# Draining a graph layer's row sums by a hand-written order on VectorE, ScalarE and GpSimd

## What is computed

```python
# graph layer, h = _ln(x)
mask = (adj > 0)
agg = mask @ h / max(sum(mask, axis=1), 1)
x = x + relu(concat(h @ W_self + b_self, agg @ W_nb + b_nb) @ W_comb + b_comb)
# mixture of experts, f = _ln(x), 8 experts, the best 2 of each row
logits = f @ Wg + bg
topk_scores, topk_idx = top_k(logits, 2);  w = softmax(topk_scores)
y_e = gelu(f @ W1[e] + b1[e]) @ W2[e] + b2[e]
x = x + sum over the two chosen e of w * y_e
```

## Time and profile before

| | |
|---|---|
| median of 3 runs | 503.56 us (502.27 to 506.07) |
| the profiled execution | 508.38 us, of it the span of the engines 505.0 us |
| busy, of the span | PE 436.5 us (86%), DVE 371.1 (73%), POOL 334.5 (66%), ACT 259.7 (51%) |
| main loop over the sums | until 335.6 us |
| drain and table | 335.6 to about 356 us |
| expert loop | about 356 to 486 us |
| last sums and writes | to 505 us |

### The profile page before, as it was taken

One profiled execution on the slowest core, in us unless ns is written; L12 is line 12 of the kernel. 1 busy time (PEld: TensorE's weight loads), 2 busy tenths in 40 slices (PEclk: granted clock), 3 DMA queues, 4 the chain that ended last, 5 costly groups with the idle time before them and its releaser, 6 DMA issues.

```text
span 505.0 us, 12812 instructions
## 1 busy us (share of the span) xinstructions
PE 436.5 (86%) x4214; PEld 384.7 (76%) x4214; DVE 371.1 (73%) x1056; ACT 259.7 (51%) x403; POOL 334.5 (66%) x348
## 2 busy tenths in 40 slices
PE   5789999889999889999979969964899999997710
PEld 5678988778888778988858858863799999996610
DVE  2898754577878977798569489766777777779972
ACT  2666872245543524344434443233588888886620
POOL 3498586165666877778658756366788788885570
PEclk9999999999999979999989979985799999999985
DMA  8997899889996999899999997196865556598665
GB/s 222 278 302 230 214 234 286 223 247 264 275 278 181 311 265 257 245 276 291 298 279 275 291 301 216 43 297 209 286 199 174 174 173 186 174 324 346 195 218 166
DMA packets 48687, 122.47 MB, mean 243 GB/s; under 512 B 10601, under 2 KB 19693, under 8 KB 47600
## 3 DMA queue, kind: packets, MB, share of 16 engines
q1 hardware_dynamic: 26736, 64.09, 44.6%
q0 software_dynamic: 16144, 50.49, 33.8%
q10 hardware_dynamic: 5744, 7.08, 5.1%
HBM read 96.52 MB, written 26.93 MB: 244 GB/s over the span
## 4 chain that ended last, share of the span: by engine, by line
DVE 34%; PE 16%; ACT 15%; DMA 13%; issue 10%; POOL 8%; ACTq 2%; DVEq 1%; POOLq 1%; SPq 0%
DMA wst<-in_L_ffn_W_dram 11%; PE bank L1245 7%; ACT stage L771 7%; DVE maskT L845 5%; DVE stage L1129 5%; ACT stage L776 4%; POOL rs L633 3%; DVE x_sb L930 2%; DVE xh L928 2%; DVE w L982 2%; DVE st L934 2%; PE bank L1236 2%; ACT xh L725 2%; PE bank L1237 2%; PE bank L1362 2%
## 5 line engine op out<-in xcount | busy, mean ns | idle before, releaser
L1236 PE MATMUL bank<-z_flat,maskT 128*128 128x257 f16 x1024 | 232.9, 278 | 8.5 <-issue 8.5
L1237 PE MATMUL bank<-z_lo,maskT 128*128 128x256 f16 x1024 | 232.7, 277 | 0.0
L1236 PEld LDWEIGHTS bank<-z_flat,maskT 128*128 128x128 fp8e4 x1024 | 101.9, 100 | 22.9 <-issue 9.0
L651 POOL DMA_INDIRECT pair_out<-rows,enum x78 | 93.6, 1199 | 33.3 <-issue 21.3
L1237 PEld LDWEIGHTS bank<-z_lo,maskT 128*128 128x128 fp8e4 x1024 | 101.8, 99 | 13.2
L676 ACT ACTIVATE mask<-stage,m 128x2048 fp8e4<-128x2048 int32 x32 | 64.1, 2002 | 58.7 <-DMA stage<-in_adj_dram,gidx 47.5
L584 POOL DMA_INDIRECT dispatched<-rows,slot x64 | 65.0, 1016 | 29.4 <-issue 18.2
L573 POOL DMA_INDIRECT stage<-in_adj_dram,gidx x64 | 65.7, 1027 | 26.1 <-issue 13.6
L633 POOL TENSOR_TENSOR rs<-ve,mhalf 128x1 f32<-128x1 f32 x32 | 39.0, 1220 | 49.9 <-DVE ve L939 49.8
L725 ACT ACTIVATE xh<-x_sb,nb,rs 128x256 f32<-128x256 f32 x32 | 19.2, 599 | 100.7 <-POOL nb L635 80.0
L1342 PE MATMUL bank<-stage,w 128*128 128x256 f16 x468 | 59.8, 279 | 4.8 <-DVE stage L1114 4.8
(11 more groups left out here) (179 smaller groups left out, 607.8 us busy)
## 6 DMA issues: line engine op xcount, KB each, us to landing
stage<-in_adj_dram SPq DMA_DIRECT2D x256, 128.0 KB, 6.4
stage<-dispatched SPq DMA_DIRECT2D x39, 260.0 KB, 3.2
wst<-in_L_ffn_W_dram ACTq DMA_DIRECT2D x16, 256.0 KB
z_lo<-pair_out SPq DMA_DIRECT2D x4, 1024.0 KB, 7.8
dispatched<-pad SPq DMA_DIRECT2D x15, 260.0 KB, 5.2
out_dram<-x_sb SPq DMA_DIRECT2D x28, 128.0 KB
maskT<-pair_out SPq DMA_DIRECT2D x3, 1024.0 KB, 9.4
x_sb<-in_x_dram ACTq DMA_DIRECT2D x6, 256.0 KB, 11.3
```

The costliest lines, as they stand in the source:

```text
L651: gp.indirect_dma_start(out=yp_dram[:, :], out_offset=bass.IndirectOffsetOnAxis(ap=enum[:, a, s:s + 1], axis=0), in_=ysb[:, a, s, :], in_o ...
L1236: mm(acc[u % 2][:, 0:D + 1], a, z_hi[:, i, :], start=(i == 0), stop=False)
L1237: last = mm(acc[u % 2][:, 0:D], a, z_lo[:, i, :], start=False, stop=(i == NT - 1))
```

## The change

The kernel's steps end at step 31 on VectorE and ScalarE and at s = 31 on GpSimd, and what is left is called in an order written by hand. The bodies of the helpers (`low`, `quotient`, `normalise_again`, `transposed`, `powers_of_row`) are those of the old steps. Line numbers of the kernel after differ from those of before by up to forty.

```diff
@@ GpSimd: powers and sends (before, lines 623 to 644)
+            def powers_of_row(t):
+                pool.wait_ge(s_ve2, t + 1)
+                gp.tensor_tensor(rs[:, t:t + 1], ve[:, t:t + 1], mhalf[:, 0:1], ALU.pow).then_inc(s_rs2, 1)
...
-            LAST_POWERS = NT + X1
-            sent = 0
-            for s in range(GATE_STEPS + 1):
-                if s > HOT and s % B == (HOT + 1) % B and (s - HOT) // B < NG - 1:
+            for s in range(NT):
+                if s > HOT and s % B == (HOT + 1) % B:
                     powers_of_e((s - HOT) // B)
-                if s == LAST_POWERS:
-                    powers_of_e(NG - 1)
-                if 0 <= s - X1 < NT:
-                    t = s - X1
+                if s >= X1:
+                    powers_of_row(s - X1)
...
-                for _ in range(1 if s < NT - B else 2):
-                    if sent < B * ((s - SLOT + (s == LAST_POWERS - 1)) // B + 1):
-                        dispatch(sent)
-                        sent += 1
+                if s >= SLOT:
+                    dispatch(s - SLOT)
+            sent = NT - SLOT
+            for t in (NT - 3, NT - 2):
+                powers_of_row(t)
+                if t == NT - 2:
+                    powers_of_e(NG - 2)
+                dispatch(sent)
+                sent += 1
+            powers_of_row(NT - 1)
+            dispatch(sent)
+            powers_of_e(NG - 1)
+            for t in range(sent + 1, NT):
+                dispatch(t)
@@ ScalarE (before, line 749)
-            steps(act, main_step, 3, NT + LOGIT, tail=1)
+            steps(act, main_step, 3, NT)
+            normalise_again(NT - 4)
+            transposed(NT - 5)
+            normalise_again(NT - 3)
+            transposed(NT - 4)
+            expert_hi(E - 1)
+            normalise_again(NT - 2)
+            transposed(NT - 3)
+            transposed(NT - 2)
+            normalise_again(NT - 1)
+            transposed(NT - 1)
@@ VectorE (before, lines 951 and 1102)
-                if t == NT + SLOT - 2 * B - 1:
-                    slots(NG - 2)
-                elif u % B == SLOT % B and live(known, SLOT) and t != NT + SLOT - 2 * B:
+                if u % B == SLOT % B and live(known, SLOT):
...
-            steps(dve, main_step, 4, NT + HOT - B + 1, tail=1)
+            steps(dve, main_step, 4, NT)
+            low(NT - 4)
+            quotient(NT - 3)
+            expert_scales(E - 1)
+            quotient(NT - 2)
+            low(NT - 3)
+            choose(NG - 2)
+            low(NT - 2)
+            quotient(NT - 1)
+            slots(NG - 2)
+            low(NT - 1)
+            expert_lo(E - 1)
+            choose(NG - 1)
@@ VectorE, ahead of the expert loop (before, line 1159)
-            for t in range(NT + HOT - B + 1, GATE_STEPS):
-                main_step(t, t, t)
+            slots(NG - 1)
```

More of the change, by code:

```diff
@@ L335, in gnn_moe_kernel @@
         EMAX, ESCALE, ESPLIT, PM = 3, 4, 5, 2
-        GATE_STEPS = NT + SLOT - B + 1
         def steps(eng, step, peel, end, total=None, tail=0):
@@ L716, in _, with normalise_again, transposed @@
             load_expert(0)
+            def normalise_again(i):
+                act.wait_ge(s_nb2, i + 1)
+                if i >= 2:
+                    act.wait_ge(s_lo2, i - 1)
+                apart(act)
+                sc.activation(xh[:, i % 2, :], flat(x_sb, i), ACT.Identity, bias=nb2[:, at(i)], scale=rs[:, at(i)]).then_inc(s_xh2, 1)
+                act.wait_ge(s_xh2, i + 1)
+                apart(act)
+                sc.copy(row16[:, at(i), 0:D].rearrange("p o d -> p (o d)"), xh[:, i % 2, :]).then_inc(s_hi2, 1)
+            def transposed(j):
+                act.wait_ge(s_tp2, j + 1)
+                if j:
+                    act.wait_ge(s_lgp, j)
+                apart(act)
+                sc.copy(xT[:, :], tp2[:, :]).then_inc(s_xT2, 1)
             def main_step(t, u, known):
                 if live(known, NORM):
[L720 to L734 removed]
+                    normalise_again(t - NORM)
+                if live(known, LOGIT):
+                    transposed(t - LOGIT)
                 if u % B == ESPLIT % B and live(known, ESPLIT):
@@ L909, in _, with low, quotient @@
                     const_row()
+            def low(i):
+                dve.wait_ge(s_hi2, i + 1)
+                v.tensor_tensor(row16[:, at(i), D:2 * D].rearrange("p o d -> p (o d)"), xh[:, i % 2, :],
+                                row16[:, at(i), 0:D].rearrange("p o d -> p (o d)"), ALU.subtract).then_inc(s_lo2, 1)
+            def quotient(j):
+                r, p = j % 4, acc[j % 2]
+                dve.wait_ge(s_mm, j + 1)
+                v.tensor_scalar(sdeg[:, r:r + 1], p[:, D:D + 1], 1.0, scw[:, 4:5], ALU.max, ALU.mult).then_inc(s_dg, 1)
+                dve.wait_ge(s_dg, 2 * j + 1)
+                v.reciprocal(rdeg[:, r:r + 1], sdeg[:, r:r + 1]).then_inc(s_dg, 1)
+                dve.wait_ge(s_sfc, j // B + 1)
+                dve.wait_ge(s_dg, 2 * j + 2)
+                v.scalar_tensor_tensor(tsum[:, r % 2, :], p[:, 0:D], rdeg[:, r:r + 1], x_row(j), ALU.mult, ALU.add).then_inc(s_ts, 1)
+                dve.wait_ge(s_ts, j + 1)
+                v.scalar_tensor_tensor(flat(x_sb, j), tsum[:, r % 2, :], 0.0, flat(x_sb, j), ALU.max, ALU.add).then_inc(s_x1, 1)
+                dve.wait_ge(s_x1, j + 1)
+                apart(dve)
+                v.bn_stats(st6[:, r, :], flat(x_sb, j)).then_inc(s_s2, 1)
+                dve.wait_ge(s_s2, 2 * j + 1)
+                apart(dve)
+                v.bn_aggr(mv2[:, r, :], st6[:, r, :]).then_inc(s_s2, 1)
+                dve.wait_ge(s_s2, 2 * j + 2)
+                v.tensor_scalar(ve[:, at(j)], mv2[:, r, 1:2], EPS, XS ** -2, ALU.add, ALU.mult).then_inc(s_ve2, 1)
             def main_step(t, u, known):
                 if live(known, NORM):
-                    i = t - NORM
-                    dve.wait_ge(s_hi2, i + 1)
-                    v.tensor_tensor(row16[:, at(i), D:2 * D].rearrange("p o d -> p (o d)"), xh[:, (u - NORM) % 2, :],
-                                    row16[:, at(i), 0:D].rearrange("p o d -> p (o d)"), ALU.subtract).then_inc(s_lo2, 1)
+                    low(t - NORM)
                 m = turned_in(t)
@@ L920, in main_step @@
                 if live(known, X1):
[L921 to L939 removed]
+                    quotient(t - X1)
                 m = made_in(t)
```

39 lines of the change are left out of this document (2 added, 37 removed).

## The result

The kernel after took 500.46 us (median of 20 runs, 495.99 to 503.11), the kernel before beside it 504.47 (20 runs). The ratio is 0.9916, with a 95% interval from 0.9892 to 0.9940: 4.2 us less, between 3.0 and 5.4. The forecast was 4.1. On two of the four chips of the experiments (e1 to e4, and e8 to e11) a stall of TensorE lengthens the expert loop of every kernel, before too, by some 17 us in some runs and some 50 in the others; a ratio there comes from the runs with the smaller stall where a kernel has more than one, and e10 and e11 have only runs with the larger.

What follows compares the result with a forecast made beforehand. The bound was taken as a drain chain through VectorE, GpSimd and ScalarE starting at late quotient 31. Gains of 3.8 + 0.3 = 4.1 us from the 503.56 median gave 499.5 us; forecast 498.3 to 501, wider range 497.2 to 503.0.

Steps and rivals of the forecast that it cites:

- three signs of being wrong: Sum 31 ending elsewhere, TensorE waiting for a load in the expert loop, or GpSimd's last scatter not 4 us earlier.
- Powers 29, 2.5 us earlier: Drain, GpSimd: with two of four sends gone ahead of them, the powers of tile 29 start 2.5 us earlier.
- Quotient 30 directly behind the scales, low part 30 ready ahead of the sum: Drain, VectorE: quotient 30 moves ahead of low part 29 to 329.4; low part 30 ends at 335.1.
- Quotient 31 at its sum, 3.8: Drain, VectorE: quotient 31 starts directly behind its sum, at 335.7 instead of 339.51, 3.8 us gained.
- Low part of the weights at no cost: Drain, VectorE: expert 7's low part, moved behind low part 31, fits in the 1.96 us wait before choice 7.
- With that cover gone it would cost 1.3: Drain, VectorE: without the wait ahead of choice 7, the low part of expert 7's weights would cost 1.3 us.
- Powers of e at the gap, 0.3: Drain, GpSimd: the last powers of e go ahead of sends and start at the logit gap; slots 7 gain 0.3 us.
- GpSimd no earlier, and nobody waits for it: Expert stage: sixteen later sends leave GpSimd no earlier; tile 9's load is in time by 0.3 us, scatter lag absorbed.
- the first rival: Expert loop: every second send held up, TensorE waits 2.4 us at tile 9, gain only 1.7, 501.9 us; 17%.
- the slower one: Expert stage: each of sixteen sends held up by a whole 0.75 us, 7.6 us lost, 511.2 us; 4%.
- takes up the 4: Near the end: GpSimd's 11.2 us of idle waiting for ScalarE absorbs the scatters' lag of some 4 us.
- The clock rival: First expert tiles: TensorE's clock rises sooner, 1.8 us more gained, 5.9 in all, 497.7 us; 13%.

Runs made afterwards that it cites:

- e1: VectorE and ScalarE in the changed kernel's order, GpSimd in the order of before; ratio to before 0.9986 (0.9940 to 1.0031).
- e4: Changed kernel with the low part of expert 7's weights moved behind the last choice; no usable ratio, slots of group 7 at 12.81 us behind sum 31.
- e8: The kernel of e1 run again for its time, on a chip with the stall; no usable ratio, quotient 31 at 3.58 us behind sum 31.
- e11: Changed kernel with unused matrix products in TensorE's drain waits and twelve more ahead of the third expert tile; ratio 1.0868, which is the stall.
- e10: Changed kernel with eight unused GpSimd powers between the last powers of e and the last sixteen sends; ratio 1.0837, which is the stall.
- e2: GpSimd in the changed kernel's order, VectorE and ScalarE in the order of before; ratio to before 1.0018 (0.9979 to 1.0058).
- e12: The kernel of e10 run again: changed kernel plus eight unused GpSimd powers ahead of the last sixteen sends; 505.70 us against 504.73, ratio 1.0022.
- e5: Changed kernel with three small unused GpSimd products ahead of the last sixteen sends; 498.70 us against 504.09, ratio 0.9914.
- e6: Changed kernel with eight small unused GpSimd products ahead of the last sixteen sends; 499.00 us against 504.09, ratio 0.9916.
- e7: Changed kernel with unused matrix products in TensorE's idle stretches of the drain and first expert step; 500.10 us against 504.09, ratio 0.9910.

## Why the prediction was right

Forecast 4.1 us less and 499.5; measured 4.2 (3.0 to 5.4) and 500.46 beside a before of 504.47. By the traces' places it is 3.78: 4.05 at the transposes of tile 2, 0.41 lost in that tile, 0.14 won behind tile 9. That forecast and measurement meet to 0.1 us is luck; that they meet within a microsecond is the chain. Of the three signs of being wrong one came true, sum 31 ends 2.6 us earlier than in before's trace, which is why all places are counted from it. TensorE waits for no load, and GpSimd's last scatter is 3.8 earlier (485.15 after 491.54 before, each from its sum 31).

1. **Powers 29, 2.5 us earlier.** Measured 2.51. e1 shows that without GpSimd's new order, of which this is the first effect, VectorE's is worth nothing.
2. **Quotient 30 directly behind the scales, low part 30 ready ahead of the sum.** In time from sum 31 I had quotient 30 at -6.2 and the start of low part 30 at -0.9; they are at -6.28 and -1.13.
3. **Quotient 31 at its sum, 3.8.** Measured 3.85. VectorE waits 0.77 for the sum, so that much is spare ahead of it. e2 shows where it comes from: the sends give 2.6 of it, VectorE's order the rest.
4. **Low part of the weights at no cost.** Right, with 0.64 of the wait left over as I had it (0.56). **"With that cover gone it would cost 1.3" was wrong**: 2.6 at the slots, 2.3 at tile 2 (e4). I had priced VectorE's time alone and had not asked who waits for the weights; it is TensorE, for its first expert tile.
5. **Powers of e at the gap, 0.3.** The slots gained 4.31 where quotient 31 gained 3.85, so 0.46, and they are at 10.25 where I had 10.5. But the transposes of tile 0 wait for neither and gained 3.83, and of the 0.46 the transposes of tile 2 kept 0.2 (4.05).
6. **GpSimd no earlier, and nobody waits for it.** The last send is 0.4 later than before. Two of the sixteen behind the powers of e are long (1.19 at 353.95 and 1.38 at 357.97, together 0.65 more than 0.96 each); the third long one (338.35) stands ahead of the wait of 1.50 and costs nothing. So the first rival's "every second send held up" didn't come true, and the 0.97 at 348.08 that I had set against the slower one says nothing, since VectorE has no instruction of line 1129 there. The tightest point, tile 9, I had in time by 0.3. It is in time by 4.2, because I took the load's issue from before, where it came 34.5 behind sum 31, and the slowest landing, 4.2; it was issued at 32.6 and landed in 2.7. Why the load followed the start of the last send by 5.7 us in before (364.44, 370.15) and by 3.4 in after isn't shown. With TensorE 0.5 later than forecast: 0.3 + 1.9 + 1.5 + 0.5 = 4.2. The rival "sends late, TensorE waits at tile 9" is a real mechanism with a threshold, and e12 shows it beyond that threshold.
   The lag of the scatters was absorbed in the wait for ScalarE, as said, but **"takes up the 4" was 3.2**: these waits fell from 11.2 us to 8.0. In the loop GpSimd doesn't catch up, as forecast, 28 tiles in 85.2 us:

```profile
POOL pair_out L658 <- ACT rows L784: 8.0, 7, 2.2
```

```profile
L658 POOL DMA_INDIRECT pair_out<-rows,enum x56 | 68.1, 1216 | 17.1 <-issue 16.8 <-ACT rows L784 0.3
```

**The clock rival** was to give 1.8 more and gave nothing; tile 2 took 0.4 more. The clock did rise sooner (at 347.3), but TensorE then stood idle around the table (0.93 and 1.05 us) and it fell again for tile 2, which took 4.74 us (349.41 to 354.15) against 4.33 before. That is the step from 4.05 to 3.64 in the table. With the same order of work there the tile took 4.74 in e5, 4.48 in e12 and 5.81 in e6, so the 0.4 is within what one execution differs from the next by, and its sign isn't shown.

What remains open: whether keeping the clock up through tile 2 gives its 1.4 us back, and what the two halves are worth in measured time rather than in places of the trace.

## What to carry to other kernels

A reordering on one engine can be worth nothing until the engine that feeds it is reordered too: follow the wait, and ask where it will stand next. When work is pushed back off the critical path, find the one consumer that gets it last and compute its slack from issue and landing, since beyond the slack one pays the wait and, as in e12, a tile at the lower clock as well. And measure a drain from the event that starts it: between two single executions the spans mixed 2.6 us from the main loop into a gain of 3.8.

## What I had not expected of the hardware

**A GpSimd send that starts more than 0.1 us inside a VectorE instruction with two inputs in SBUF ends some 0.86 us behind it.** e12 shows it cleanly, because its scatters drift past VectorE's line 1172 (the line 1129 of before). First VectorE, then GpSimd:

```profile
384.42 0.75 DVE L1172 SCALAR_TENSOR_TENSOR stage<-stage,shs 128x512 f16<-128x512 f32 x1 [1.63 <-ACT stage L803]
387.48 0.75 DVE L1172 SCALAR_TENSOR_TENSOR stage<-stage,shs 128x512 f16<-128x512 f32 x1 [0.72 <-ACT stage L803]
390.55 0.75 DVE L1172 SCALAR_TENSOR_TENSOR stage<-stage,shs 128x512 f16<-128x512 f32 x1 [0.72 <-ACT stage L803]
```

```profile
384.11 0.99 POOL L661 DMA_INDIRECT pair_out<-rows,enum  x1 [0.30 <-issue]
...
387.99 1.11 POOL L661 DMA_INDIRECT pair_out<-rows,enum  x1 [0.30 <-issue]
...
390.69 1.47 POOL L661 DMA_INDIRECT pair_out<-rows,enum  x1 [0.30 <-issue]
...
393.76 1.47 POOL L661 DMA_INDIRECT pair_out<-rows,enum  x1 [0.30 <-issue]
```

The scatter at 384.11 starts before VectorE's instruction and takes its usual 0.99, though it overlaps it. The one at 387.99 starts inside (387.48 to 388.23) and ends at 389.10; that at 390.69 starts inside (390.55 to 391.30) and ends at 392.16. Both end 0.87 and 0.86 behind. From 390.69 on every second scatter is caught, two take 3.07 us, and that is TensorE's time for a tile: the two engines lock. This is why the mean of a scatter was 1.229 in the earlier trace rows, and why GpSimd, which could make two in 2.58 us, doesn't catch up by 0.5 us a tile. Between 369.89 and 386.69, where VectorE's instruction first is missing (TensorE waits) and then never has a scatter start inside it, fourteen scatters in a row took 0.99 to 1.00 each.

It isn't any VectorE instruction that does it. Line 1162 of after has one of its two tiles in PSUM (`bank`), and the scatter at 375.02, inside it (374.74 to 375.48), took 0.99. A `tensor_tensor` with both inputs in SBUF does it too: the longest scatter of after, 1.87 at 480.40, starts inside one of 1.21 at 480.20 and ends 0.86 behind it. And a send that starts in the first 0.1 us of line 1169 isn't held up; VectorE's instruction is then a little longer. VectorE, then GpSimd, in after:

```profile
360.84 0.80 DVE L1169 SCALAR_TENSOR_TENSOR stage<-stage,shs 128x512 f16<-128x512 f32 x1 [0.73 <-ACT stage L800]
```

```profile
360.92 0.96 POOL L583 DMA_INDIRECT dispatched<-rows,slot  x1 [0.30 <-issue]
```

The Trainium skill (SBUF — State Buffer, "Who interferes with whom") says that a VectorE instruction with two SBUF inputs contends with a GpSimd instruction that reads SBUF, and that whichever issues first holds the port while the other waits. The rows agree on the first, and on the second where VectorE is first. Where the scatter is first they don't: VectorE's instruction at 384.42 starts inside the scatter of 384.11, takes its usual 0.75, and starts 0.14 behind the end of the ScalarE instruction that it waits for, as the one at 390.55 does with no scatter beside it. The 3.1 us that the Trainium skill has for a send starved of descriptor writes (SBUF — State Buffer, "A bandwidth-pool intuition that's wrong (but worth ruling out)") are seen in no row here.

**TensorE's clock falls for less than I thought.** Idle stretches of 1.49 and 1.02 us around a single short product were followed by 0.50 in e7 (347.3 to 350.6, the first part of tile 2), and 5.13 us of waiting by 0.50 for most of tile 9 in e12. In both it was back at the upper level for the next tile.
